# Graph and expert layers on one core: order and start of GpSimd's gathers and products in the edge stage

## The chip, the cores and the metric

The kernel runs on one core of one Trainium2 chip. The metric is the device time of one execution in microseconds (us). One core has five engines with their own instruction queues: TensorE (PE in the profile; PEld are its weight loads), VectorE (DVE), ScalarE (ACT), GpSimd (POOL) and SyncE (SP, which issues DMAs). They meet through semaphores: an instruction raises one when it is done, and a wait holds everything behind it on its own engine.

## The reference

Four layers are added one after another to `x` (1250 nodes, 512 features), each on the layer norm of `x`: a segment mean, a dense top-2-of-8 mixture of experts, a graph layer over 40,000 edges, and a dropless mixture of 8 experts. The change is in the graph layer, which in short is:

```
x0, x1 = node features (128 scalars, 128 vectors of 3), projected by W_up0, W_up1
h   = three SiLU layers over 8 edge features;  w1..w4 = split(h @ W_mlp4)      # 4 x 128 per edge
s0, s1 = x0[sender], x1[sender];  y0, y1 = edge_attr[:, 0], edge_attr[:, 1:4]
p1 = w1*s0*y0;  p2 = (w2*s0) y1;  p3 = w3*s1*y0;  p4 = w4 * <s1, y1> / sqrt(3)
msg = segment_sum over the receiving node of [p1, p4] and [p2, p3]
out = [msg0 @ W_out0, msg1 @ W_out1] / 10
```

## The kernel before, in words

The edges lie sorted by receiver in `NTILE` = 352 tiles of 128. The edge stage takes them in `STEPS` = 88 steps of `Q` = 4 tiles. The projected rows of all nodes lie in a table in HBM (`node_table`, 2 KB a row). For a tile, GpSimd gathers the 128 rows of its senders (256 KB) with an indirect DMA (`gather(i)`, L1950). There are `NGAT` = 8 places for gathered tiles, so a gather may start once the tile that lay there eight tiles ago has been used.

What the engines do in step s, each in the order written out in its own function:

- TensorE makes the products `h @ W_mlp4` of the step's tiles (`weights_of`, L1735), some MLP products for later tiles (L1689 to L1702), then the sum over receivers of the step before (`sum_up(s - 1)`, L1749 and L1752), which raises `p_sum` to s. `sum_up` waits for all messages of its step (`v_msg` from VectorE, `g_msg` from GpSimd), for ScalarE's picks and for VectorE's close before (`v_sum`).
- ScalarE copies the first half of the fourth tile's weights out of PSUM (`copy_weights`, L1400, `a_wcopy`), runs MLP functions (L1324 to L1336) and writes the picks (L1392), the one-hot rows scaled by the edge attributes.
- VectorE makes the messages (`messages_of`): the products with s0 of the first two tiles (L1029), each tile's products with s1 (L1036, raises `v_msg`), and the same for the other two, where the fourth tile's s0 product is left to GpSimd. It waits for the gathered rows. Then `close(s - 1)` (L1048) adds TensorE's sum to the running sum, after a wait for `p_sum`. Once in four steps it makes compares for the picks (L1015).
- GpSimd issues gathers two steps ahead and makes the fourth tile's s0 product (`products_of(s)`, L1939, raises `g_msg`), after waits for `a_wcopy`, for that tile's gather and for `p_sum` at s - 1.
- SyncE stores each running sum to HBM (L2140), 512 KB a step.

GpSimd's order before: eight gathers; then in each step the gathers of tiles 4s + 8 and 4s + 9, the product of step s, and the gathers of tiles 4s + 10 and 4s + 11. A gather of tile i waits for `v_msg` at i - 7, and every fourth one for the product of two steps before its own tile (`g_msg`).

Of the kernel before, what the change touches and what calls it, by code (L numbers as in the profile page):

```python
# [41 lines left out]
Q = 4  # L42
BT = 8
NTILE = -(-((NE - NW) // TILE + NW) // BT) * BT
STEPS = NTILE // Q
# [108 lines left out]
def program(nc, consts, x, anc, sub, leaf_table, src, dst, ea4, ea8, gate, w13, w2, w_up, w_mlp1, w_mlp23,  # L154
            w_mlp4, w_out, ew, ei, v1, v2, out):
    ctx = ExitStack()
    with ctx:

        def sem(name):
            return ctx.enter_context(nc.semaphore(name))  # L160
# [235 lines left out]
        p_prod, p_tp, p_sum = sem("mlp_product"), sem("edge_weights"), sem("step_summed")  # L396
# [1461 lines left out]
        def gpsimd(g):  # L1858
# [73 lines left out]
            def products_of(s):  # L1932

                i = s * Q + Q - 1
                g.wait_ge(a_wcopy, s + 1)
                g.wait_ge(d_gat[i % NGAT], 16 * (i // NGAT + 1))
                if s >= 2:
                    g.wait_ge(p_sum, s - 1)
                g.tensor_tensor(out=msg_pair[s % 2 * 2 + 1][:, 1, 0:2],  # L1939
                                in0=w_copy[s % 2].rearrange("p (w u) -> p w u", w=2),  # L1940
                                in1=gat_pair[i % NGAT // 2][:, 1, 0:1].to_broadcast([128, 2, MUL]), op=ALU.mult
                                ).then_inc(g_msg, 1)

            def gather(i):
                if i >= NGAT:
                    g.wait_ge(v_msg, i - NGAT + 1)
                    if i % Q == Q - 1:
                        g.wait_ge(g_msg, (i - NGAT) // Q + 1)
                row = gat_pair[i % NGAT // 2][:, i % 2].rearrange("p m u -> p (m u)")
                g.indirect_dma_start(out=row, out_offset=None, in_=table,  # L1950
                                     in_offset=bass.IndirectOffsetOnAxis(ap=senders[:, i:i + 1], axis=0)
                                     ).then_inc(d_gat[i % NGAT], 16)
# [5 lines left out]
            g.wait_ge(g_packed, 6)  # L1958
            for i in range(NGAT):
                gather(i)  # L1960
            for s in range(STEPS + 1):
                for i in range(s * Q + NGAT, s * Q + NGAT + Q):
                    if i < NTILE:
                        gather(i)
                    if i % Q == 1 and s < STEPS:
                        products_of(s)


            g.wait_ge(v_sumrow, 1)
# [194 lines left out]
        block.scalar(scalar)  # L2164
        block.tensor(tensor)
        block.gpsimd(gpsimd)
        block.sync(sync)

# [48 lines left out]
```

## Time and profile before

| | us |
|---|---|
| timed runs, median of 3 | 1487.02 (1486.22 to 1489.55) |
| profiled execution, span from first to last instruction | 1615.3 |
| VectorE, ScalarE, GpSimd busy in the profiled execution | 1216.0, 1023.7, 987.3 |
| edge stage in it | about 840 to 1477 |

The profiled execution has no time of its own beside its span; durations in the trace belong to it and not to the timed runs. "Idle before" is the engine's idle time ahead of an instruction, followed by what ended it; "issue" is time in which it waited for nothing that the trace shows, and "remote" is a semaphore's rise for which the trace has no instruction near enough. TensorE's ends are modelled from its starts.

### The profile page before, as it was taken

To read this page: it belongs to the slowest core of one execution; us is meant where nothing else is said; L and a number is where in the kernel's file an instruction comes from. 1 tells how busy PE (TensorE), PEld (TensorE's weight loads), DVE (VectorE), ACT (ScalarE), POOL (GpSimd) and SP (SyncE) were. 2 spreads that over 40 slices of the span, in tenths; PEclk is the share of its full clock that TensorE was granted. 3 is DMA by queue.
4 is the path that set the end of the run, shared out by engine and by line. 5 is a ranking of instruction groups with operands and counts; after the bars stand their busy time and mean duration, and the time that the engine had idled before them with its cause. 6 is when DMAs were issued, how large, how long until landed. Compare 5 with 4: busy or idle time off the path is not lost. (4 is left out here: it accounts for less than half of the span.)

```text
span 1615.3 us, 26230 instructions
## 1 busy us (share of the span) xinstructions
PE 1427.6 (88%) x8774; PEld 853.3 (53%) x8774; DVE 1216.0 (75%) x1633; ACT 1023.7 (63%) x2442; POOL 987.3 (61%) x850
## 2 busy tenths in 40 slices
PE   5938999999999999999877888888788888878999
PEld 3626648882888478856552333333333333334787
DVE  7887739991999389947947887778888788785655
ACT  6337638871888378846465776677677677773443
POOL 4155658888888887888616666656666666663000
PEclk9858999999999999999988989989999989999999
DMA  9355492777459585561446677766777768775421
GB/s 326 116 222 175 124 383 32 258 256 254 101 184 336 178 266 157 191 192 18 102 179 201 220 229 223 222 207 216 224 232 213 229 211 240 221 222 178 146 103 55
DMA packets 91614, 316.66 MB, mean 196 GB/s; under 512 B 23754, under 2 KB 25988, under 8 KB 80859
## 3 DMA queue, kind: packets, MB, share of 16 engines
q1 hardware_dynamic: 45832, 202.57, 33.4%
q0 software_dynamic: 45648, 112.41, 27.5%
q8 instruction: 71, 1.16, 0.3%
q14 instruction: 63, 0.52, 0.1%
HBM read 378.96 MB, written 77.16 MB: 282 GB/s over the span
## 5 line engine op out<-in xcount | busy, mean ns | idle before, releaser
L1903 POOL DMA_INDIRECT sorted_edges<-arena x320 | 474.8, 1484 | 113.8 <-issue 99.3
L1950 POOL DMA_INDIRECT arena<-node_table,arena x352 | 337.8, 960 | 256.3 <-DVE arena L1036 152.2
L905 DVE TENSOR_TENSOR weights_hl<-arena,weights_hl 128x1024 fp32r<-128x1024 f32 x342 | 405.3, 1223 | 64.2 <-ACT weights_hl L1234 60.4
L1234 ACT ACTIVATE weights_hl<-arena 128x1024 fp32r<-128x1024 f32 x342 | 352.0, 1060 | 47.7 <-PE pair L1596 47.2
L1392 ACT ACTIVATE arena<-arena 128x32 f32<-128x32 bf16 x1408 | 359.3, 344 | 2.1 <-DVE arena L1015 2.1
L1596 PE MATMUL pair<-weights_hl,rows_hl 128*128 128x512 f32 x1368 | 327.9, 397 | 4.6 <-ACT weights_hl L1234 3.0
L1036 DVE TENSOR_TENSOR arena<-pair,arena 128x768 f32<-128x768 f32 x352 | 319.1, 949 | 0.0
L1596 PEld LDWEIGHTS pair<-weights_hl,rows_hl 128*128 128x128 f32 x1368 | 253.2, 189 | 70.6 <-DVE weights_hl L905 10.0
L1735 PE MATMUL pair<-arena 64*128 64x512 f32 x704 | 197.9, 630 | 22.3 <-issue 12.3
L1048 DVE SCALAR_TENSOR_TENSOR arena<-arena,pair 128x1024 f32<-128x1024 f32 x88 | 112.6, 1280 | 115.2 <-remote 102.0
L1596 PE MATMUL pair<-weights_hl,hidden_hl 128*128 128x512 f32 x684 | 165.7, 395 | 0.0
L1752 PE MATMUL pair<-arena 128*32 128x256 f32 x2112 | 151.4, 422 | 0.2 <-issue 0.2
L1596 PEld LDWEIGHTS pair<-weights_hl,hidden_hl 128*128 128x128 f32 x684 | 124.9, 188 | 25.6
L1752 PEld LDWEIGHTS pair<-arena 128*32 128x32 f32 x2112 | 81.9, 123 | 101.6 <-issue 79.4
L1749 PE MATMUL pair<-arena 128*32 128x512 f32 x704 | 110.7, 703 | 20.0 <-DVE arena L1048 18.0
L1735 PEld LDWEIGHTS pair<-arena 64*128 64x128 f32 x704 | 65.2, 188 | 106.4 <-issue 102.5
L924 DVE TENSOR_TENSOR arena<-pair,arena 128x512 f32<-128x512 f32 x69 | 47.3, 686 | 97.5 <-PE pair L1633 47.8
L1702 PE MATMUL pair<-arena 64*64 64x256 f32 x704 | 69.3, 437 | 53.2 <-ACT arena L1328 48.9
L1029 DVE TENSOR_TENSOR arena<-pair,arena 128x512 f32<-128x512 f32 (+1 forms) x176 | 97.0, 551 | 17.4 <-DMA arena<-node_table,arena 9.5
L1272 ACT ACTIVATE arena<-pair 128x512 f32<-128x512 f32 x69 | 41.4, 599 | 97.5 <-PE pair L1633 83.0
L1328 ACT ACTIVATE arena<-pair 128x512 f32<-128x512 f32 x44 | 26.3, 598 | 112.1 <-remote 90.2
L1633 PE MATMUL pair<-arena 128*64 128x512 f32 x352 | 87.0, 603 | 0.0
(287 smaller groups left out, 1564.8 us busy)
## 6 DMA issues: line engine op xcount, KB each, us to landing
arena<-in_w SPq DMA_DIRECT2D x73, 2048.0 KB
arena<-in_w SPq DMA_DIRECT2D x85, 1024.0 KB
sums<-arena SPq DMA_DIRECT2D x88, 512.0 KB
other_down<-in_w SPq DMA_DIRECT2D x8, 1024.0 KB
arena<-in_v SPq DMA_DIRECT2D x16, 512.0 KB, 4.1
pair_rows<-arena SPq DMA_DIRECT2D x1, 5934.0 KB
arena<-pair_rows SPq DMA_DIRECT2D x23, 256.0 KB
arena<-node_table,arena POOLq DMA_INDIRECT x352
```

The source lines that it names most:

```text
L905: v.tensor_tensor(out=part[s][:, 1], in0=by_chunk(n)[4], in1=part[s][:, 0].bitcast(F32), op=ALU.subtract).then_inc(v_low, 1)
L1029: v.tensor_tensor(out=m[:, 0:n, 0:2], in0=tp[:, :].rearrange("p (t w u) -> p t w u", t=2, w=4)[:, 0:n, 0:2], in1=rows_in[:, 0:n, 0:1].to_b ...
L1036: v.tensor_tensor(out=m[:, t, 2:8].rearrange("p (w m) u -> p w m u", w=2), in0=w34.unsqueeze(2).to_broadcast([128, 2, 3, MUL]), in1=rows_i ...
L1048: v.scalar_tensor_tensor(out=run_sum[s % NSUM], in0=run_sum[(s - 1) % NSUM], scalar=g_same[:, s:s + 1], in1=sum_pair[:, :], op0=ALU.mult, ...
L1234: a.activation(out=part[s][:, 0], in_=cols, func=ACT.Copy).then_inc(a_high, 1)
L1392: done = a.activation(out=picks[s % NPICK][:, j, c], in_=hot[s // HOT_STEPS % NHOT][:, :, s % HOT_STEPS, j], func=ACT.Copy, scale=recs[:, ...
L1596: mm = pe.matmul(out=bank[:, :], lhsT=st[:, a], rhs=part[s][:, w, half * 512:(half + 1) * 512], start=begins and (a, w) == (0, 0), stop=en ...
L1735: pe.matmul(out=tp_bank[(i + h) % Q], lhsT=act3[batch % 2][p, k * 128:(k + 1) * 128], rhs=m4_sb[p], start=True, stop=True).then_inc(p_tp, 1)
L1749: mm = pe.matmul(out=bank, lhsT=pick, rhs=m[:, 1:5], start=True, stop=True, skip_group_check=True)
L1752: mm = pe.matmul(out=bank.rearrange("p (b u) -> p b u", b=4)[:, c - 1:4:4 - c], lhsT=pick, rhs=m[:, 0:c + 5:c + 4], start=c == 1, stop=Tru ...
L1903: g.indirect_dma_start(out=sorted_edges, out_offset=bass.IndirectOffsetOnAxis(ap=slot_i[:, j:j + 1], axis=0), in_=er[:, j, :], in_offset=N ...
L1950: g.indirect_dma_start(out=row, out_offset=None, in_=table, in_offset=bass.IndirectOffsetOnAxis(ap=senders[:, i:i + 1], axis=0)).then_inc( ...
```

## The change

In each step GpSimd first makes the product of step s, then (except in the first step) waits until TensorE's sum of step s - 1 is done (`p_sum` at s), and then issues the four gathers of tiles 4s + 8 to 4s + 11 one after the other. The waits inside `gather` and `products_of` are as before.

```diff
             for i in range(NGAT):
                 gather(i)
-            for s in range(STEPS + 1):
+            for s in range(STEPS):
+                products_of(s)
+                if s:
+                    g.wait_ge(p_sum, s)
                 for i in range(s * Q + NGAT, s * Q + NGAT + Q):
                     if i < NTILE:
                         gather(i)
-                    if i % Q == 1 and s < STEPS:
-                        products_of(s)
```

## Rows read from the trace of the kernel before

**Rows 1.** The page's head and busy times: us, share of the span, instructions.

```profile
span 1615.3 us, 26230 instructions
...
PE 1427.6 (88%) x8774; PEld 853.3 (53%) x8774; DVE 1216.0 (75%) x1633; ACT 1023.7 (63%) x2442; POOL 987.3 (61%) x850
```

**Rows 2.** Busy us (and instructions) of each engine by stretch, then TensorE's clock, DMA share, GB/s.

```profile
500.00:824.00 324.00, 308.90 (x1439) 216.76 (x1437) 243.25 (x269) 204.70 (x248) 244.44 (x167) 0.98 0.56 174
...
868.00:1473.50 605.50, 508.95 (x4417) 199.25 (x4411) 491.32 (x618) 425.21 (x1585) 384.35 (x421) 0.92 0.71 220
```

**Rows 3.** Groups by line and form, VectorE, 868 to 1473.5 us: busy us, mean ns | idle before.

```profile
L1048 DVE SCALAR_TENSOR_TENSOR arena<-arena,pair 128x1024 f32<-128x1024 f32 x86 | 110.0, 1280 | 106.7 <-remote 96.0 <-PE pair L1752 10.3 <-issue 0.4
L1029 DVE TENSOR_TENSOR arena<-pair,arena 128x512 f32<-128x512 f32 x85 | 58.3, 686 | 7.4 <-PE pair L1735 5.4 <-issue 0.9 <-remote 0.4
```

**Rows 4.** Groups by line, ScalarE, same stretch.

```profile
L1328 ACT ACTIVATE arena<-pair 128x512 f32<-128x512 f32 x41 | 24.5, 598 | 104.8 <-remote 83.8 <-PE pair L1695 20.5 <-issue 0.4
```

**Rows 5.** Timeline of TensorE: start us, us, instruction, count, idle before and releaser.

```profile
1450.09 1.48 PE L1752 MATMUL pair<-arena 128*32 128x256 f32 x24
```

**Rows 6.** Timeline of VectorE, the stage's last steps.

```profile
1447.33 1.27 DVE L1048 SCALAR_TENSOR_TENSOR arena<-arena,pair 128x1024 f32<-128x1024 f32 x1
...
1456.71 1.28 DVE L1048 SCALAR_TENSOR_TENSOR arena<-arena,pair 128x1024 f32<-128x1024 f32 x1 [3.71 <-remote]
...
1462.30 1.27 DVE L1048 SCALAR_TENSOR_TENSOR arena<-arena,pair 128x1024 f32<-128x1024 f32 x1
1463.48 0.68 DVE L1029 TENSOR_TENSOR arena<-pair,arena 128x512 f32<-128x512 f32 x1
...
1465.82 0.41 DVE L1029 TENSOR_TENSOR arena<-pair,arena 128x256 f32<-128x256 f32 x1
...
1467.88 1.27 DVE L1048 SCALAR_TENSOR_TENSOR arena<-arena,pair 128x1024 f32<-128x1024 f32 x1
```

**Rows 7.** Timeline of VectorE, a regular step.

```profile
1107.74 1.28 DVE L1048 SCALAR_TENSOR_TENSOR arena<-arena,pair 128x1024 f32<-128x1024 f32 x1 [0.22 <-PE pair L1752]
1108.94 0.42 DVE L1015 TENSOR_TENSOR arena<-arena 128x512 bf16<-128x512 bf16 x1
1109.27 0.68 DVE L1029 TENSOR_TENSOR arena<-pair,arena 128x512 f32<-128x512 f32 x1
```

**Rows 8.** Timeline of GpSimd, one whole round.

```profile
1447.87 0.98 POOL L1950 DMA_INDIRECT arena<-node_table,arena  x1 [0.16 <-POOL arena L1939]
...
1450.42 0.95 POOL L1950 DMA_INDIRECT arena<-node_table,arena  x1 [0.30 <-DVE arena L1036]
1451.68 0.95 POOL L1950 DMA_INDIRECT arena<-node_table,arena  x1 [0.30 <-issue]
1452.65 0.73 POOL L1939 TENSOR_TENSOR arena<-edge_weights,arena 128x256 f32<-128x256 f32 x1
1453.54 0.98 POOL L1950 DMA_INDIRECT arena<-node_table,arena  x1 [0.16 <-issue]
1454.82 0.96 POOL L1950 DMA_INDIRECT arena<-node_table,arena  x1 [0.30 <-issue]
```

**Rows 9.** Timeline of all engines, a step without a hold.

```profile
1463.70 0.39 ACT L1400 ACTIVATE edge_weights<-pair 128x256 f32<-128x256 f32 x1 [0.21 <-PE pair L1735]
1463.71 1.06 PE L1749 MATMUL pair<-arena 128*32 128x512 f32 x8
...
1464.57 1.50 PE L1752 MATMUL pair<-arena 128*32 128x256 f32 x24
```

**Rows 10.** Timeline of ScalarE, a step with MLP work.

```profile
1450.12 0.36 ACT L1400 ACTIVATE edge_weights<-pair 128x256 f32<-128x256 f32 x1
```

**Rows 11.** Timeline of VectorE and GpSimd at the stage's start.

```profile
841.62 0.99 POOL L1950 DMA_INDIRECT arena<-node_table,arena  x1 [0.30 <-issue]
...
847.88 0.69 DVE L1029 TENSOR_TENSOR arena<-pair,arena 128x512 f32<-128x512 f32 x1 [9.49 <-DMA arena<-node_table,arena]
```

**Rows 12.** Timeline of GpSimd, a pause within a round.

```profile
1230.05 0.96 POOL L1950 DMA_INDIRECT arena<-node_table,arena  x1 [2.19 <-DVE arena L1036]
```

## The prediction

> **What bounds the kernel now.** I read the busy shares first, then busy time by stage, then the edge stage's groups by line, then single steps in the timeline. In [rows 1] the reader sees a span of 1615.3 us with TensorE busy for 88% of it, so the stages must be taken apart. The timed runs have a median of 1487.02 us (1486.22 to 1489.55): the profiled execution is 128.3 us longer than the runs that I have to forecast. So the first question is which waits of this trace exist in the timed runs.
>
> [Rows 2] cut the span. The dense experts (500 to 824 us) have TensorE busy 308.9 of 324.0 us: little there could be shorter without a profile. The edge stage, 605.5 us, has VectorE busy 491.3 and GpSimd 384.4. In [rows 3] 86 closes (L1048) fall into it, 7.04 us a step. VectorE works without a pause inside a step; its idle time stands before the close, 106.7 us (96.0 of it "remote", which no instruction in the trace explains), and before the first message, 7.4. [Rows 4] show ScalarE held in the same way for 83.8 us before one of the MLP's layers (L1328): both wait for TensorE's semaphores.
>
> A wait looks like this: TensorE's sums have run at 1450.09, lasting 1.48 us [rows 5], yet the close that waits for them starts at 1456.71 after 3.71 us idle [rows 6]. In the last steps, as the gathers run out, closes start at 1462.30 and 1467.88, 5.58 us apart, with no wait at all [rows 6]. The compares (L1015) add 0.33 us (1108.94 to 1109.27 in [rows 7]) once in four steps, 0.08 a step: VectorE's floor is 5.66 us.
>
> GpSimd is just as full when it isn't held. In [rows 8] its round in the present order goes from 1447.87 to 1453.54, 5.67 us: four gathers of 0.95 to 0.98, three gaps of 0.30, one of 0.16 and a product of 0.73.
>
> **Which of the waits are in the timed runs.** Without the 114.1 us in which VectorE idled (106.7 and 7.4) the profiled execution would have taken 1501.2 us. The timed median is 14 us below even that. Since TensorE leaves at most 15 us of the 324 in the dense stage, the 128 us must come mainly from the edge stage: 86 steps at 7.04 less 5.66 give 119. I conclude that the timed runs step at VectorE's floor, and that the long holds come with the profiling. The Trainium skill ("Runtime: NRT & Kernel Launch", The ~15µs preamble/postamble breakdown) says that a profile's total is some 6.2 us over the execution time that the runtime reports, whatever the kernel. By that 122 us would be left to explain, still the edge stage's 119; no run here shows the 6.2.
>
> **The change part by part.** I take a step in which nothing is held, with its close at time 0: 1462.30 in [rows 6]. The messages start at 1.18 (1463.48). TensorE's sum, which waits for that close, runs from 1.41 to 3.77 (1463.71 to 1464.57 + 1.50 in [rows 9]). The copied weights are ready at 1.79 (1463.70 + 0.39), or at 3.15 with MLP work ahead of them (1450.12 + 0.36, less 1447.33, [rows 6, 10]).
>
> *Gathers now.* The first waits for the step's first message and starts at 3.09 (1450.42 less the close at 1447.33), the others at 4.35, 6.21 and 7.49; the product stands at 5.32 to 6.05 [rows 6, 8].
>
> *Gathers after.* They wait for the sum's end at 3.77. With the 0.30 that every released gather shows they start at 4.1, 5.35, 6.6 and 7.9, at 1.26 apart. Their own waits for messages (the fourth message ends at 5.6) are over when their turns come. The fourth also needs its step's product, which lies ahead of it now. So they are issued 1.0, 1.0, 0.4 and 0.4 us later. What hides this is the distance to their use: gathers of one step fill rows that are read two steps later, first pair at 11.3 + 1.2 = 12.5, second at 11.3 + 3.5 = 14.8. A landing isn't in the trace by itself, so I bound it: eight gathers in a row start the stage, and VectorE is released at 847.88 by the second, started at 841.62, so landing takes at most 6.3 us from the start, and at least the gather's own 0.99 [rows 11]. I take the upper end, since bursts are what the change makes: second gather 11.65 against 12.5, fourth 14.2 against 14.8. Both fit, with 0.9 and 0.6 us left (1.9 and 1.0 before). Cost 0. Should landing take over 7 us, the cover is gone (below).
>
> The Trainium skill ("DMA: Bandwidth & Descriptors", Anatomy of one DMA — SWDGE (gpsimd) path) puts a DMA issued by GpSimd at about 2.0 us plus its bytes over 436 GB/s. For a gather of 256 KB that is an estimate of 2.6 us, and the fourth gather would have 4.3 us to spare instead of 0.6; the sum is 0 by both.
>
> *The product moved first.* The same 88 products of 0.73 us [rows 8]. It waits for the copied weights (1.8 to 3.2) and for GpSimd, which leaves its last gather at 7.9 + 0.97 = 8.9, that is 3.2 in the next step. It ends at 4.0 instead of 6.05. TensorE needs it only at 1.4 of the next step (7.1), so being 2 us earlier gains nothing where nothing was late. Behind it on GpSimd's queue stand the four gathers alone, and SyncE's queue isn't touched.
>
> *The added wait.* Behind it stand the four gathers; for them wait messages two steps on. It is one more semaphore between product and first gather. Nothing in this trace shows that pair. The gap there is 0.16 after a product now and 0.30 after a gather; so it costs between -0.02 (the 0.02 gap before a product) and +0.14 a step. I take 0, nearest to the 0.16: a round of 5.05 + 0.73 less overlaps is the same 5.67 us, against VectorE's 5.66. Over 86 steps the ends are -2 and +12 us. At both ends of the loop (eight gathers ahead; the last step's sum, which is long over when the stage's end waits for its stores) nothing is added.
>
> Sum: 0 us on a timed run, so 1487.0. The profiled execution may move far more than that: the added wait keeps two of four gathers out of TensorE's sum, and the holds appear only where gathers do. Its 1615.3 could fall to 1501 with no timed run any shorter.
>
> **Rivals.** *The holds are partly real* (faster). For it: regular steps, too, begin with a wait of 0.22 us for a sum that had ended ([rows 7]), and these waits vanish with the gathers. Against: the accounting above leaves no room. If a wait of that size is in each of the timed runs' steps, and as much again in some, say 0.25 us a step, and the change takes it out, 86 steps give 21 us: 1466.
>
> *GpSimd becomes the bound* (slower). Its round of 5.67 stands beside VectorE's 5.66, and now it must begin at a sum's end: whatever delays a sum is lost to GpSimd. Place: the gap between product and first gather. With the price 0.14 its round is 5.81, and 86 times 0.14 are 12 us: 1499. It decides when the round passes 5.66 by more than some 0.01 a step, since the 0.6 us of spare landing time are then used up within the stage. For it: such a pause of GpSimd as the 2.19 us in [rows 12] is not caught up. Against: the product is 2 us early now, so a late GpSimd hurts TensorE less.
>
> *Landing is the limit* (slower). From close to fourth gather, landing and the second pair's 2.06 us of messages, three steps must hold 7.9 + landing + 2.06; this passes 3 x 5.66 at a landing of 7.0 us, before the change at 7.4. Where it is over both, the cost is 0.4 us in three steps, 12 us in all: 1499. Against: at most 6.3 in a burst of eight; for it, the stores of sums share the DMA engines, at 0.71 busy in the stage [rows 2].
>
> *The change doesn't do what it says.* Where GpSimd is late, the sum is already over when it asks, and only the product's place is changed: 1487.
>
> **How the numbers follow.** My forecast with the last rival, 0.52. Holds partly real, 0.24. GpSimd's bound 0.14 and landing 0.10. A difference counts from 0.2% (3 us), about what a measurement can tell. So faster 0.24, same 0.52, slower 0.24. The range for 8 in 10 reaches into both sides: 1466 (21 us) to 1500 (12 us and a little for the runs' own spread). The likeliest case alone has 1484 to 1490.
>
> **What would show it.** After the change each product stands ahead of four gathers in one block, the first about 4.1 us after a close, and the product ends some 3 us before TensorE's sum. If VectorE's step in the profile is near 5.7 us and the time is unchanged, the holds belonged to the profile. If the message lines (L1029) wait for gathers, landing was the limit. If GpSimd shows no gap of more than 0.30 in its round while VectorE idles, GpSimd bounds. The prediction fails if the timed runs did have the holds: then the time drops by tens of us, and the accounting from the two totals is wrong.

## The result, and the profile after

The change made the kernel slightly slower: 1492.5 us median of 8 runs (1487.8 to 1496.7) against 1486.62 of 8, a ratio of 1.0037 (95% interval 1.0019 to 1.0055). Two later comparisons of the same kernel gave 1.0014 (0.9994 to 1.0033) and 1.0009 (0.9995 to 1.0022). Weighted by their intervals the three make 1.0018 (1.0009 to 1.0027), 2.7 us; this takes their errors as independent. The three lie further apart than their intervals would have it, and the two later ones include 1, so that a small cost is likely, smaller than the first comparison said, and its size is less sure than the pooled interval.

The page after, and the row of its part 6 (KB, median us from issue to landing):

```profile
span 1493.5 us, 26316 instructions
...
PE 1373.5 (92%) x8774; PEld 831.8 (56%) x8774; DVE 1208.0 (81%) x1633; ACT 1028.8 (69%) x2442; POOL 982.6 (66%) x850
...
L1048 DVE SCALAR_TENSOR_TENSOR arena<-arena,pair 128x1024 f32<-128x1024 f32 x88 | 115.9, 1318 | 3.7 <-PE pair L1752 3.6
...
arena<-node_table,arena POOLq DMA_INDIRECT x352, 5.2
```

The profiled execution after has a span of 1493.5 us and took 1495.31 us, 1.8 more. The holds of [rows 3, 4] are gone: 3.7 us idle before all 88 closes. That is no merit of the change. The kernel before, profiled once more, doesn't have them either. Its page:

```profile
span 1484.7 us, 26230 instructions
...
arena<-node_table,arena POOLq DMA_INDIRECT x352, 4.7
```

So the 1615.3 us of [rows 1] were those of one single execution, and this second profile is the one to compare with. Under L1036, the first and last message of the edge stage (first and last start, us), before again and then after:

```profile
L1036 DVE TENSOR_TENSOR arena<-pair,arena x352: 935/935/950, 841.4 to 1340.3; 128x768 f32<-128x768 f32 x176
```

```profile
L1036 DVE TENSOR_TENSOR arena<-pair,arena x352: 943/968/1118, 845.5 to 1348.2; 128x768 f32<-128x768 f32 x176
```

By these starts the stage took 498.9 us before and 502.7 with the change; the change's other two profiles have 500.8 and 501.3. One profile each can't carry the difference: kernels below that the timed runs don't tell from the kernel before have 497.8 to 501.7. Where VectorE waits in it, up to 1345 us (the longest wait of each first line is for the stage's first rows, before the order differs), before again and after:

```profile
DVE arena L1029 <- DMA arena<-node_table,arena: 11.5, 2, 10.9
DVE arena L1029 <- issue: 1.8, 2, 1.5
DVE arena L1029 <- PE pair L1735: 0.4, 1, 0.4
```

```profile
DVE arena L1029 <- DMA arena<-node_table,arena: 13.8, 4, 11.0
DVE arena L1029 <- issue: 3.4, 5, 1.1
DVE arena L1029 <- PE pair L1735: 1.2, 3, 0.7
```

Without that first wait it is 2.8 us before (0.6, 1.8 and 0.4) and 7.4 after (2.8, 3.4 and 1.2), all at L1029, the instruction that waits for gathered rows (and, in the last line of each view, for TensorE's weights). Rows that come late are part of what separates the two, but not all of it is the added wait's: the change's other profiles have 4.4 and 3.9 us, and three profiles of its order with the wait left out or holding nothing (below) have 5.2, 3.2 and 4.5.

What the change's three profiles share, and neither before again nor these three have, is a wait for rows at the start of step 11 (VectorE's steps counted from 0), 0.4 to 0.6 us. After:

```profile
908.10 0.69 DVE L1029 TENSOR_TENSOR arena<-pair,arena 128x512 f32<-128x512 f32 x1 [0.44 <-DMA arena<-node_table,arena]
```

GpSimd in the regular stretch, before again and after, to be laid beside [rows 8]:

```profile
1010.52 0.98 POOL L1950 DMA_INDIRECT arena<-node_table,arena  x1 [0.16 <-POOL arena L1939]
...
1014.32 0.94 POOL L1950 DMA_INDIRECT arena<-node_table,arena  x1 [0.30 <-DVE arena L1036]
1015.27 0.75 POOL L1939 TENSOR_TENSOR arena<-edge_weights,arena 128x256 f32<-128x256 f32 x1
1016.18 0.98 POOL L1950 DMA_INDIRECT arena<-node_table,arena  x1 [0.16 <-POOL arena L1939]
```

```profile
1155.44 0.74 POOL L1939 TENSOR_TENSOR arena<-edge_weights,arena 128x256 f32<-128x256 f32 x1
1156.37 0.98 POOL L1950 DMA_INDIRECT arena<-node_table,arena  x1 [0.18 <-issue]
1157.64 0.96 POOL L1950 DMA_INDIRECT arena<-node_table,arena  x1 [0.30 <-DVE arena L1036]
1158.91 0.95 POOL L1950 DMA_INDIRECT arena<-node_table,arena  x1 [0.31 <-issue]
1160.16 0.95 POOL L1950 DMA_INDIRECT arena<-node_table,arena  x1 [0.30 <-DVE arena L1036]
1161.12 0.74 POOL L1939 TENSOR_TENSOR arena<-edge_weights,arena 128x256 f32<-128x256 f32 x1
1162.02 0.98 POOL L1950 DMA_INDIRECT arena<-node_table,arena  x1 [0.16 <-issue]
```

Both rounds are full: 1010.52 to 1016.18 is 5.66 us, 1156.37 to 1162.02 is 5.65. In the new order the product stands ahead of four gathers, and no gap is over 0.31. VectorE's closes there are 5.58 apart, as in [rows 6], and 5.66 with the compares shared out. So there is next to no time in a round to catch anything up. What the wait adds shows where TensorE's sum is late, above all at the stage's start:

```profile
852.15 0.73 POOL L1939 TENSOR_TENSOR arena<-edge_weights,arena 128x256 f32<-128x256 f32 x1
854.89 0.98 POOL L1950 DMA_INDIRECT arena<-node_table,arena  x1 [2.01 <-PE pair L1752]
856.17 0.95 POOL L1950 DMA_INDIRECT arena<-node_table,arena  x1 [0.30 <-issue]
```

GpSimd stood idle for 2.01 us until TensorE's first sum; in the change's other profiles this wait is 1.42 and 3.06 us. From there a step's first gather starts 5.0 to 5.9 us after VectorE's last message for some ten steps, against 3.4 to 4.0 in before again (and 3.8 to 4.4 or 4.5 to 5.4 in the two profiles with the product first and no wait), and the wait for rows at step 11 follows.

### The profile page after: what moved, and what is told of

It is laid out like the page before. It is cut to its first block, busy times and chain, and to the rows that moved or that the text cites. A ratio compares the mean times of both kernels' runs of the same rounds, so it can differ in the third digit from the quotient of the medians.

```text
span 1493.5 us, 26316 instructions
## 1 busy us (share of the span) xinstructions
PE 1373.5 (92%) x8774; PEld 831.8 (56%) x8774; DVE 1208.0 (81%) x1633; ACT 1028.8 (69%) x2442; POOL 982.6 (66%) x850
## 4 chain that ended last, share of the span: by engine, by line
PE 39%; DMA 31%; POOL 15%; issue 7%; DVE 7%; ACT 1%; SPq 0%; DVEq 0%; POOLq 0%; ACTq 0%
DMA arena<-node_table,arena 27%; PE pair L1596 21%; POOL sorted_edges L1903 9%; POOL arena L1950 3%; PE pair L1633 3%; PE pair L1842 3%; PE pair L1853 3%; PE pair L1650 2%; PE pair L1587 1%; POOL pair_rows L1893 1%; PE pair L1796 1%; DMA node_sums<-arena 1%; POOL node_sums L1913 1%; DVE arena L1036 1%; DMA other_up1b<-in_w 1%
## 5 line engine op out<-in xcount | busy, mean ns | idle before, releaser
L1036 DVE TENSOR_TENSOR arena<-pair,arena 128x768 f32<-128x768 f32 x352 | 326.8, 992 | 0.0
L1752 PE MATMUL pair<-arena 128*32 128x256 f32 x2112 | 130.8, 379 | 0.0
L1735 PEld LDWEIGHTS pair<-arena 64*128 64x128 f32 x704 | 56.7, 187 | 124.6 <-ACT arena L1328 48.0
L1029 DVE TENSOR_TENSOR arena<-pair,arena 128x512 f32<-128x512 f32 (+1 forms) x176 | 104.5, 594 | 18.5 <-DMA arena<-node_table,arena 13.8
L1752 PEld LDWEIGHTS pair<-arena 128*32 128x32 f32 x2112 | 72.2, 110 | 80.5 <-issue 52.7
L1272 ACT ACTIVATE arena<-pair 128x512 f32<-128x512 f32 x69 | 41.3, 599 | 99.0 <-PE pair L1633 84.2
L1749 PE MATMUL pair<-arena 128*32 128x512 f32 x704 | 94.8, 610 | 1.3
L1913 POOL DMA_INDIRECT node_sums<-arena x27 | 51.6, 1912 | 43.0 <-ACT arena L1280 25.9
L1939 POOL TENSOR_TENSOR arena<-edge_weights,arena 128x256 f32<-128x256 f32 x88 | 65.3, 742 | 9.7 <-ACT edge_weights L1400 3.9
```

Of the source, the lines that this page charges most:

```text
L1029: v.tensor_tensor(out=m[:, 0:n, 0:2], in0=tp[:, :].rearrange("p (t w u) -> p t w u", t=2, w=4)[:, 0:n, 0:2], in1=rows_in[:, 0:n, 0:1].to_b ...
L1036: v.tensor_tensor(out=m[:, t, 2:8].rearrange("p (w m) u -> p w m u", w=2), in0=w34.unsqueeze(2).to_broadcast([128, 2, 3, MUL]), in1=rows_i ...
L1735: pe.matmul(out=tp_bank[(i + h) % Q], lhsT=act3[batch % 2][p, k * 128:(k + 1) * 128], rhs=m4_sb[p], start=True, stop=True).then_inc(p_tp, 1)
L1752: mm = pe.matmul(out=bank.rearrange("p (b u) -> p b u", b=4)[:, c - 1:4:4 - c], lhsT=pick, rhs=m[:, 0:c + 5:c + 4], start=c == 1, stop=Tru ...
```

## The experiments

"Ratio" is to the kernel before, timed beside each run, with its 95% interval. In the expectations, theory A (first "theory 1") says that only the time at which the first gathers may start counts, since GpSimd's round is as full as VectorE's.

**Without the wait.** The product's place alone.

```diff
                 products_of(s)
-                if s:
-                    g.wait_ge(p_sum, s)
```

> The product stands first in the step as in the change, but GpSimd does not wait for TensorE's sum. Theory 1 (late gathers: the wait holds the first two gathers of a step until 4.5 us after a close instead of some 3.1 to 4, and those whose landing takes over 6 us then reach VectorE late): without the wait this is the kernel before, 1486.6 us within 2. Theory 2 (the wait costs as an instruction in a full round of GpSimd): also 1486.6. Theory 3 (the product's new place costs, beside VectorE's work): as slow as the change, 1492.5. In the profile of this kernel I expect the long holds of TensorE's semaphore back if it was the wait that kept them away, and a span near 1490 if it was the product's place.

> Product first without the wait, a second time, partner of the run before: 1485 to 1488, level with the kernel before or up to 2 us under it.

Measured: 1487.11 us, ratio 0.9988 (0.9972 to 1.0005), and again 1486.71, 0.9996 (0.9981 to 1.0011). Its spans, 1490.9 and 1486.5, show no holds: the wait didn't keep them away. In time the product's place is free, and what costs is the wait. The change ran beside the second of these:

> The change a third time, beside the same order without the wait (next run). Theory A: 1.5 to 5 us over the next run, as the profiles' waits for rows say (4.7 and 7.4 us with the change, 2.8 in the old order). If the first comparison was a chance, the two are level.

Measured 1489.02 us, 1.0009 (0.9995 to 1.0022): 2.3 us over its partner. The profile has 3.9 us of waits at L1029 after the stage's first.

VectorE's timelines show where the parts act. Its steps 10 and 80 (the first is step 0) begin here, with the wait and then in the partner without it:

```profile
897.10 0.69 DVE L1029 TENSOR_TENSOR arena<-pair,arena 128x512 f32<-128x512 f32 x1
...
1296.43 0.68 DVE L1029 TENSOR_TENSOR arena<-pair,arena 128x512 f32<-128x512 f32 x1
```

```profile
899.22 0.69 DVE L1029 TENSOR_TENSOR arena<-pair,arena 128x512 f32<-128x512 f32 x1
...
1296.30 0.70 DVE L1029 TENSOR_TENSOR arena<-pair,arena 128x512 f32<-128x512 f32 x1
```

| us, one number for each profile | steps 10 to 80 | steps 80 to 87 |
|---|---|---|
| old order: before again; with a wait at the third gather, which holds nothing | 400.8; 401.0 | 39.0; 39.3 |
| product first, no wait (twice); with a wait at the third gather | 398.3, 397.1; 397.8 | 42.2, 41.3; 42.7 |
| the change, three times | 400.5, 399.4, 399.3 | 42.2, 41.5, 40.6 |

In the long stretch the wait costs 1.0 to 3.4 us against its own order, in line with the timed 2.3. (In the ten steps before it the three groups overlap, 56.2 to 58.5 us.) The product's place is free only in sum: it saves some 3 us there and loses 1 to 4 in the last steps, where rows come late in this order with the wait or without it. A good part of the saving is that GpSimd's products no longer run beside VectorE's compares (see the heavier round below).

**The wait in the old order**, ahead of the first gather.

```diff
             for s in range(STEPS):
+                if s:
+                    g.wait_ge(p_sum, s)
                 for i in range(s * Q + NGAT, s * Q + NGAT + Q):
                     if i < NTILE:
                         gather(i)
                     if i % Q == 1:
                         products_of(s)
```

> The old order (two gathers, product, two gathers) with the wait for TensorE's sum ahead of the first gather. Theory 1: as slow as the change or slower, since the first gather starts at the same 4.5 us and the product now stands behind two late gathers: from a sum's end 0.26 to the gather, 2.23 to the product, 0.73 for it and 2.4 for the next sum make a loop of some 5.7 to 5.8 us against VectorE's 5.66: 1493 to 1503. Theory 2: 1492. Theory 3: 1486.6.

Measured: 1494.48 us, 1.0033 (1.0017 to 1.0049), as theory 1 has it, at the low end. The loop closes. Its timelines of GpSimd and of TensorE:

```profile
1067.05 0.94 POOL L1950 DMA_INDIRECT arena<-node_table,arena  x1 [0.36 <-PE pair L1752]
...
1069.26 0.74 POOL L1939 TENSOR_TENSOR arena<-edge_weights,arena 128x256 f32<-128x256 f32 x1
...
1072.75 0.94 POOL L1950 DMA_INDIRECT arena<-node_table,arena  x1 [0.35 <-PE pair L1752]
```

```profile
1070.10 1.07 PE L1749 MATMUL pair<-arena 128*32 128x512 f32 x8 [0.84 <-issue]
1070.96 1.50 PE L1752 MATMUL pair<-arena 128*32 128x256 f32 x24
```

The product ends at 1070.00, TensorE's sum starts at 1070.10 after an idle 0.84 us, and the gather that waits for it at 1072.75: a round of 5.70 us. With the product first, as in the change, a product stands behind the wait of the round before, so this loop spans two steps and should have room to spare; that is argued from the order and not tried by itself.

**The wait where it holds nothing**, ahead of the third gather: in the new order and in the old.

```diff
                 for i in range(s * Q + NGAT, s * Q + NGAT + Q):
+                    if s and i % Q == 2:
+                        g.wait_ge(p_sum, s)
                     if i < NTILE:
                         gather(i)
```

> Product first, then two gathers without the wait, then the wait for TensorE's sum, then the other two gathers. The third gather has its turn at 6.2 us or later, when the sum (3.8 to 4.2) is long over, so the wait exists and holds nothing. Theory 1: 1486.6 within 2. Theory 2 (cost of the wait itself): 1490 to 1493. Theory 3: 1492.5.

> The old order with the wait for TensorE's sum ahead of the third gather, where it holds nothing in a run without holds. Theories 1 and 3: 1486.6 within 2. Theory 2: 1490 to 1493. The profile tells of the holds: if they need gathers during TensorE's sum, they are back (span near 1600), and each now stops the third and fourth gather too.

Measured: 1.0002 (0.9989 to 1.0015) and 0.9998 (0.9984 to 1.0012), spans 1484.2 and 1484.9 us. The wait as an instruction costs nothing; it must hold something back.

**Other things to wait for**, later or earlier than the sum, in the change's place. TensorE isn't asked.

```diff
                 if s:
-                    g.wait_ge(p_sum, s)
+                    g.wait_ge(v_msg, s * Q + 2)     # or + 3, or + 4
```

> As the change, but the wait ahead of the step's first gather is for VectorE's second message of the step instead of TensorE's sum. Theory A (what counts is the time at which the first gather may start; GpSimd's round is as full as VectorE's, so time it idles comes back as late rows, whatever it waits for): the first gather can start at 3.9 us after the last message, against 4.0 to 4.5 with the sum and 3.8 to 4.4 when only the round is full, so little is lost: 1487 to 1491, clearly less than the change. Theory B (it is TensorE's semaphore, its coupling or its wake-up, that costs): as the kernel before, 1487 to 1488. They part only weakly here and strongly in the next.

> As the change, but waiting for VectorE's third message: the first gather can start at 4.9 us, between the sum's 4.0 to 4.5 and the fourth message's 5.9. Theory A (only the time of the first gather counts): between their 1492 and 1522, nearer to the lower: the four waits at 3.9, 4.0 to 4.5, 4.9 and 5.9 lie on one rising curve: 1493 to 1503. Theory B (TensorE's coupling costs): 1486 to 1488, since no sum is waited for; the fourth message then would have been a case of its own.

> As the change, but the wait is for the fourth message, with which VectorE ends the step: the first gather starts at 5.9, the fourth at 9.7 us. TensorE's sum is not waited for. Theory A: three steps must hold 9.7 + landing + 2.06 us; with landings of 5.2 (median) to 7.7 that is 5.65 to 6.5 us a step against 5.66, so VectorE waits for rows in many steps: 1500 to 1530. Theory B: 1487 to 1488.

| the step's first gather not before, us after the last message, by the profiles | ratio |
|---|---|
| 4.0 (two messages) | 0.9977 (0.9954 to 1.0001), 1485.98 us |
| 4.2 to 4.55 (the sum: the change, three times) | 1.0037, 1.0014, 1.0009 |
| 5.1 (three messages; 4.9 expected) | 1.0022 (1.0002 to 1.0042), 1491.21 us |
| 5.9 (four messages) | 1.0238 (1.0208 to 1.0268), 1522.18 us |

Theory B is out: a wait that has nothing to do with TensorE costs the more the later it ends. But it isn't the smooth curve that I expected: up to 5.1 us the cost is 0.2% or so (1491.21 us, under my 1493), and 0.8 us later it is 2.4%. The wait for two messages came out under both theories' ranges; in its profile the first gathers start no earlier and hardly later than without a wait, so it is close to a third run of the product first alone. In the last one's VectorE timeline

```profile
1043.68 1.28 DVE L1048 SCALAR_TENSOR_TENSOR arena<-arena,pair 128x1024 f32<-128x1024 f32 x1
1046.56 0.69 DVE L1029 TENSOR_TENSOR arena<-pair,arena 128x512 f32<-128x512 f32 x1 [1.60 <-issue]
```

and its waits show rows that come late at some 40 places in the 88 steps (the first wait, 9.4 us, is the stage's own):

```profile
DVE arena L1029 <- DMA arena<-node_table,arena: 20.2, 17, 9.4
DVE arena L1029 <- issue: 15.4, 25, 1.6
```

**A lighter round for GpSimd.** The product is cut to a copy of the weights; the factor of the gathered row is left out. With the change's order, and with the old one.

```diff
-                g.tensor_tensor(out=msg_pair[s % 2 * 2 + 1][:, 1, 0:2],
-                                in0=w_copy[s % 2].rearrange("p (w u) -> p w u", w=2),
-                                in1=gat_pair[i % NGAT // 2][:, 1, 0:1].to_broadcast([128, 2, MUL]), op=ALU.mult
-                                ).then_inc(g_msg, 1)
+                g.tensor_copy(out=msg_pair[s % 2 * 2 + 1][:, 1, 0:2],
+                              in_=w_copy[s % 2].rearrange("p (w u) -> p w u", w=2)).then_inc(g_msg, 1)
```

> The change, with the fourth tile's product cut to a copy of the weights (the factor of the gathered row is left out), which shortens GpSimd's round by an estimated 0.3 us and leaves order and wait as they are. Theory A: the round has slack now, pauses of GpSimd are caught up, and only the wait's own floor of 4.0 to 4.5 is left: most of the 5 us is gone, within 2 us of the old order with the same light product. Theory C (the fixed delay of the first two gathers is all; a full round has no part in it): still 4 to 6 us over the old order with the light product.

> The kernel before with the same light product (the factor of the gathered row is left out), the partner of the run before this one. Theory A: GpSimd's pauses near steps 26, 52 and 79 are caught up, VectorE waits less for rows: 1483 to 1487. Theory C: VectorE's floor is the limit already, 1486.6 to 1488.5, no gain.

Measured: 1486.15 us, 0.9988 (0.9971 to 1.0006), with the change; 1483.63, 0.9977 (0.9959 to 0.9996), in the old order. GpSimd's timeline in the latter:

```profile
1006.90 0.40 POOL L1939 COPY arena<-edge_weights 128x256 f32<-128x256 f32 x1
1007.47 0.98 POOL L1948 DMA_INDIRECT arena<-node_table,arena  x1 [0.17 <-DVE arena L1036]
...
1010.26 0.95 POOL L1948 DMA_INDIRECT arena<-node_table,arena  x1 [0.55 <-DVE arena L1036]
```

The copy takes 0.40 us instead of 0.73, and GpSimd now waits 0.55 us for VectorE. The old order gains, as theory A has it: after GpSimd's pause near step 52 its first gathers come back from 4.7 us after the last message to 3.1 within six steps. But the gain has a second source, since VectorE's compares aren't lengthened in this profile (see the heavier round). The change is 2.5 us over its partner, a little more than theory A's 2 and less than C's 4 to 6, and within the error of what it costs with the full round. So this pair doesn't tell theory A from C by the difference, and by the gain only in part.

**A heavier round**, in the old order: one small fill behind the product, then four.

```diff
                         products_of(s)
+                        g.memset(ap=filler[:, s:s + 1], constant=0.0)     # then four, each to a place of its own
```

> The kernel before with one more small instruction of GpSimd in each step, a fill of 128 x 1 behind the product (some 0.12 us and a gap: a round of some 5.8 to 5.85 us instead of 5.67). Nothing waits for it but GpSimd's own next gather. Theory A (GpSimd's round is already as full as VectorE's): 0.13 to 0.18 us in each of 88 steps, less the 3 us of lag that the rows can take first: 1494 to 1502. Theory C (GpSimd has room, VectorE alone is the limit): 1487 within 2.

> The kernel before with four small fills of GpSimd (128 x 1, 0.11 us each) behind the product in each step. By the run with one fill they overlap a little and hide in the gap once: an estimated 0.2 to 0.35 us more a round, 5.87 to 6.0 instead of 5.67. Theory A (GpSimd's round is as full as VectorE's): 88 times that, less some 3 us of lag: 1501 to 1515. Theory C (GpSimd has room): 1487 within 2.

Measured: 1.0001 (0.9981 to 1.0022) with one. It was no test: the fill fits into the gap behind the product and lengthened the round by some 0.02 us. With four, 1494.42 us, 1.0061 (1.0038 to 1.0083). Its GpSimd timeline:

```profile
1006.20 0.20 POOL L1969 MEMSET arena<- 128x1 f32 x4
1006.55 0.97 POOL L1951 DMA_INDIRECT arena<-node_table,arena  x1 [0.15 <-issue]
...
1012.31 0.98 POOL L1951 DMA_INDIRECT arena<-node_table,arena  x1 [0.15 <-issue]
```

The round is 5.76 us (1006.55 to 1012.31), only 0.10 longer than before, less than the 0.2 that I had estimated. 88 times 0.10 is 9 us; 8.5 were measured, against the 14 to 28 of my expectation. Nothing but GpSimd's next gather waits for a fill, so GpSimd's round was already a limit in the kernel before.

That the loss comes through late rows isn't shown by this run. Its waits for rows and weights after the stage's first are 3.3 us, hardly more than the 2.8 before. What grew are VectorE's compares (L1015, here L1016), before again and with four fills, 868 to 1340 us:

```profile
L1015 DVE TENSOR_TENSOR arena<-arena 128x512 bf16<-128x512 bf16 x19 | 9.8, 517 | 0.0
```

```profile
L1016 DVE TENSOR_TENSOR arena<-arena 128x512 bf16<-128x512 bf16 x19 | 12.9, 680 | 0.0
```

A compare takes about 0.42 us where GpSimd makes no product beside it. In the second profile of the kernel before the two meet, and both take longer:

```profile
1227.12 0.63 DVE L1015 TENSOR_TENSOR arena<-arena 128x512 bf16<-128x512 bf16 x1
```

```profile
1227.35 0.98 POOL L1939 TENSOR_TENSOR arena<-edge_weights,arena 128x256 f32<-128x256 f32 x1
```

The product takes 0.74 us elsewhere. In the old order the lateness of GpSimd's round brings its product (or its fills) beside the compare: from step 55 on in before again, behind GpSimd's pause, and in most of the stage with four fills. Counted from a compare's start to VectorE's next (0.33 us where the two don't meet), the stage's 20 compares cost 2 us more than that in before again, 5 us more with four fills, and 0.4 us or less in the profiles of the change and of its order without the wait. Why the two slow each other wasn't tried.

**The kernel before and the change, profiled again.**

> The kernel before, profiled once more. Five orders, with and without the wait, have shown no hold of TensorE's semaphores in their profiles. If the holds belong to the old order under the profiler, the span is again near 1615 us; if they were that one execution's, it is 1484 to 1492, as the others'.

> The change once more, in one call with the next two, for a fair comparison and a second profile: ratio to the kernel before 1.002 to 1.005, 1490 to 1495 us. GpSimd's first gather again never starts less than 4.0 us after the last message, and VectorE waits more than 5 us for rows in the stage.

Measured: a span of 1484.7 us (above), and for the change 1489.82 us, 1.0014 (0.9994 to 1.0033), just under the low end of what I expected; 4.4 us of waits at L1029 after the stage's first instead of the 5 or more.

**A try at a better version**: no wait, and a load moved out of the stage's start.

```diff
-            load_second(0)
             s.wait_ge(v_sum, 1)
...
+                if i == 8:
+                    load_second(0)
```

> A try at a version better than both: product first without the wait, and the 1 MB load of the last stage's first weights issued after the ninth store instead of just ahead of the edge stage, where it lands beside the first eight gathers. If that load delays the first rows, VectorE's wait for them (9.4 to 11.0 us in the profiles) falls by 1 to 2.5 us: 1484 to 1487. If the gathers alone set it, 1486 to 1488.

Measured: 1488.4 us, 1.001 (0.999 to 1.003), over what I expected. VectorE's first wait did fall, to 6.8 us, but its later waits at L1029 came to 7.6, about half of that in the steps right behind the ninth store: the load seems only to have moved to where its traffic delays other rows. No version here that computes the same is shown to beat the kernel before; the wait for two messages (0.9977) comes nearest.

## Why the prediction was wrong

*Which waits are real.* Right, and by the two totals alone: the timed runs have none of the holds, and 86 steps at VectorE's floor fit. Wrong was to put them down to profiling: of eighteen profiled executions one had them. What caused them there stays open. The Trainium skill ("Runtime: NRT & Kernel Launch", The ~15µs preamble/postamble breakdown) has 6.2 us for a profile's total over the reported time. The span here, from first to last instruction, isn't that total; it lies 1.8 us under the time of its execution, and no run shows the 6.2.

*Gathers after, "Cost 0"*: this is the step that failed, and with it the 0 for the added wait. I worked out one step in which nothing is late and took it for all 86. There I had 4.1 us for the first gather. Between steps 34 and 70 the traces show 4.3 to 4.9, but the same order without the wait has 4.3 to 4.9 there as well: the full round sets it, not the wait. The wait holds where a sum is late: at the stage's start GpSimd lost 1.4 to 3.1 us to the first sum, which a round of 5.65 us beside VectorE's 5.66 can't catch up, so that the first gathers stood at 5.0 to 5.9 for ten steps and VectorE waited for rows at step 11 in each of the three profiles. That accounts for 0.4 to 0.6 us; the rest of the 1.0 to 3.4 in the table above is spread over single steps that differ from profile to profile, and its causes aren't shown one by one.

And I took 6.3 us, from one burst at the stage's start, as the upper end of landing. After, the landing times of all gathers:

```profile
DMA to landing us min/median/max: 3.3/5.2/7.7
```

GpSimd and VectorE near the stage's end:

```profile
1331.99 0.95 POOL L1950 DMA_INDIRECT arena<-node_table,arena  x1 [0.30 <-issue]
1333.24 0.94 POOL L1950 DMA_INDIRECT arena<-node_table,arena  x1 [0.31 <-DVE arena L1036]
```

```profile
1341.37 0.42 DVE L1029 TENSOR_TENSOR arena<-pair,arena 128x256 f32<-128x256 f32 x1 [2.04 <-DMA arena<-node_table,arena]
```

Third and fourth gather of a step start at 1331.99 and 1333.24, and VectorE is released at 1341.37: 8.1 us for the later one, well over the 7.0 at which I had put the point of decision (counted, as there, from the gather's start to VectorE's). A stall at the same place stands in the profiles of the new order without the wait (1.6 us) and with the wait at the third gather (1.7), so this one isn't the wait's own; but with such a tail a delay can cost something in any step. The estimate of 2.6 us by the Trainium skill ("DMA: Bandwidth & Descriptors", Anatomy of one DMA — SWDGE (gpsimd) path) is half the median measured here.

*GpSimd's bound.* The mechanism that I gave 0.14 is half of the answer: the round is full, and "whatever delays a sum is lost to GpSimd" is what the trace shows at the stage's start. But its place and its price were wrong. The gap behind the product stayed at 0.16 (0.18 at most in the rows above), so the round didn't grow, and the 0.14 a step on which the price rested isn't there. The price of 12 us was more than four times too high.

*The product moved first.* I said that it gains nothing. In sum that holds, by luck: it keeps GpSimd's product away from VectorE's compares, which I hadn't seen, and it loses about as much in the last steps.

*The holds are partly real.* No: 0.

*The number.* I said 1487.0, and up to 0.2% no change. The pooled 2.7 us lie just inside that bound, the first comparison's 5.9 outside. The failing was less in the size than in the sign: for a wait put before work whose queue has no slack, zero is an end of the range and not its middle.

## What to carry to other kernels

When one engine bounds a loop, compare the rounds of the others with it before a wait is added: a queue that is just as full can't catch up what it waits. Follow a late start through the steps behind it, and not one step in which nothing is late. Judge the lateness that a prefetch can bear by the tail of its landings, not by one case or the median. Measure the parts of a change apart: a total near zero can be a gain and a loss. And when a profiled execution is much longer than the timed runs, profile it again before any row of it is believed.

## What the runs showed of the hardware

GpSimd pauses by itself for up to 2 us at the same steps in most profiles. In the old order it does so near steps 26 and 52 in all seven profiles, and near step 79 in all but one. With the change it pauses near 26 and 79 and not near 52; with the product first and no wait, only near 79. In the second profile of the kernel before:

```profile
991.70 0.94 POOL L1950 DMA_INDIRECT arena<-node_table,arena  x1 [1.05 <-DVE arena L1036]
```

```profile
1143.96 0.96 POOL L1950 DMA_INDIRECT arena<-node_table,arena  x1 [2.19 <-DVE arena L1036]
```

```profile
1295.85 0.94 POOL L1950 DMA_INDIRECT arena<-node_table,arena  x1 [1.20 <-DVE arena L1036]
```

VectorE, named as releaser, had long been done (2 us earlier, when the pause near 52 began). What pauses GpSimd, and why the order moves it, wasn't tried.
